# The variance matmul of a fused middle stage, moved behind the first tile of the block's second feed-forward product

## What is computed

```python
# end of layer 0
X = Q + ctx @ W_o
h = relu(X @ w1.T + b1)
x = h @ w2.T + b2 + X            # the kernel's y
# beginning of layer 1
mu = mean(x, axis=-1)
var = mean(square(x - mu), axis=-1)
q = ((x - mu) * rsqrt(var + 1e-5) * gamma + beta) @ Wq.T
```

## Time and profile before

| | |
|---|---|
| median of three runs | 6007.33 us |
| profiled execution | 6018.56 us, span of its trace 6016.6 us |
| busy share of the span: TensorE, VectorE, ScalarE, GpSimd | 92%, 63%, 53%, 44% |
| `middle` in the trace | from about 1741 us to 2137 us |
| mean granted TensorE clock | 0.956 |

### The profile page before, as it was taken

One profiled execution on the slowest core, in us unless ns is written; L12 is line 12 of the kernel. 1 busy time (PEld: TensorE's weight loads), 2 busy tenths in 40 slices (PEclk: granted clock), 3 DMA queues, 4 the chain that ended last, 5 costly groups with the idle time before them and its releaser, 6 DMA issues. The chain is left out here.

```text
span 6016.6 us, 104478 instructions
## 1 busy us (share of the span) xinstructions
PE 5513.0 (92%) x28932; PEld 3458.3 (57%) x28932; DVE 3760.4 (63%) x6550; ACT 3171.1 (53%) x5833; POOL 2621.9 (44%) x1284
## 2 busy tenths in 40 slices
PE   5959999999979979999999999999999995489999
PEld 4834444444437746666565656656566663367877
DVE  4448887778846667777777777777777773511111
ACT  3327776667743346666666666666666662122222
POOL 0000000000000049999999999999999992000000
PEclk9969998999989989999999999999999997799999
DMA  3441111111124321111111111111111115710000
GB/s 107 119 110 29 32 35 32 33 32 36 28 78 124 107 65 40 39 29 38 40 40 40 39 38 30 40 38 39 41 40 28 40 26 161 237 37 14 28 28 14
DMA packets 322981, 323.19 MB, mean 54 GB/s; under 512 B 183136, under 2 KB 187104, under 8 KB 320480
## 3 DMA queue, kind: packets, MB, share of 16 engines
q1 hardware_dynamic: 322528, 317.82, 20.1%
HBM read 210.79 MB, written 106.82 MB: 53 GB/s over the span
## 5 line engine op out<-in xcount | busy, mean ns | idle before, releaser
L750 DVE TENSOR_REDUCE a_maxes<-a_mscore 128x1 f32<-128x458 f32 (+4 forms) x5632 | 3052.8, 605 | 1031.1 <-PE a_mscore L787 1025.7
L733 ACT ACTIVATE a_prob<-a_score 128x512 f32<-128x512 f32 x4992 | 2595.9, 604 | 1402.2 <-PE a_score L796 1391.0
L787 PE MATMUL a_mscore<-a_k,a_qm 96*128 96x458 f32 (+4 forms) x5632 | 2074.6, 416 | 68.8 <-DMA a_k<-k 56.4
L796 PE MATMUL a_score<-a_q,a_k 97*128 97x512 f32 (+1 forms) x4992 | 2061.9, 436 | 76.4 <-ACT a_prob L733 51.8
L703 POOL TENSOR_TENSOR a_added<-a_added,a_prob 128x1024 f32<-128x1024 f32 x768 | 1831.9, 2385 | 90.5 <-ACT a_prob L733 34.1
L787 PEld LDWEIGHTS a_mscore<-a_k,a_qm 96*128 96x128 f32 (+1 forms) x5632 | 1577.7, 309 | 213.8 <-DVE a_maxes L750 92.5
L815 PE MATMUL a_acc<-a_prob,a_v 128*32 128x512 f32 x9984 | 1617.6, 611 | 0.0
L796 PEld LDWEIGHTS a_score<-a_q,a_k 97*128 97x128 f32 (+1 forms) x4992 | 948.9, 194 | 1133.8 <-ACT a_prob L733 599.1
L700 POOL TENSOR_TENSOR a_added<-a_prob 128x1024 f32<-128x1024 f32 x128 | 304.6, 2380 | 2267.6 <-ACT a_prob L733 2267.3
L810 PE MATMUL a_acc<-a_prob,a_ones 128*1 128x512 f32 x2048 | 965.2, 593 | 0.0
L1118 DVE TENSOR_TENSOR f_hl<-f_h,f_hh 128x512 fp32r<-128x512 f32 x128 | 88.6, 692 | 588.0 <-ACT f_hh L1097 588.0
(11 more groups left out here) (183 smaller groups left out, 3842.9 us busy)
## 6 DMA issues: line engine op xcount, KB each, us to landing
a_qm<-q SPq DMA_DIRECT2D x384, 64.0 KB, 1.9
a_q<-q SPq DMA_DIRECT2D x384, 64.0 KB, 1.9
acc<-a_acc_sb SPq DMA_DIRECT2D x384, 64.0 KB
o_part<-acc SPq DMA_DIRECT2D x24, 1024.0 KB, 10.8
a_k<-k SPq DMA_DIRECT2D x48, 416.0 KB, 5.8
q<-m_qout SPq DMA_DIRECT2D x128, 128.0 KB, 2.3
k<-kv_out SPq DMA_DIRECT2D x30, 512.0 KB, 2.7
a_qm<-q SPq DMA_DIRECT2D x384, 32.0 KB, 1.8
```

Of the source, the lines that this page charges most:

```text
L733: act.activation(prob[:, t], score[SCORES[it.j][t]][:], ACT.Exp, scale=SCALE).then_inc(exp_done, 1)
L750: dve.tensor_reduce(maxes[j][:, t, c:c + 1], mscore[u % UNIT_BANKS][:, 0:wide], AX.X, ALU.max).then_inc(unit_read, 1)
L787: pe.matmul(mscore[u % UNIT_BANKS][:, 0:wide], qm[j][r:r + ROW, t:NB:NB // P], kt[kk][r:r + ROW, at:at + wide], start=True, stop=True).the ...
L796: pe.matmul(score[SCORES[it.j][t]][:], kt[it.k][r:r + C, i * P:(i + 1) * P], qt[it.j][r:r + C, :], start=True, stop=True).then_inc(score_d ...
```

## The change

In TensorE's program `project` takes a list of tiles. The first tile of `project(n)` is issued directly behind `hidden(n)`; the waits for `sqsum_done` and for the square root of the block before, and the variance matmul, follow it; then the other three tiles. The other engines' programs are untouched.

```diff
-            def project(n):
+            def project(n, tiles):
                 if n == 0:
                     pe.wait_ge(w_lo, 3)
-                for d in range(KT):
+                for d in tiles:
                     products(prod[d], W2, d, (lambda k: hh[:, k], lambda k: hl[:, k]), HT,
                              (lambda k: pe.wait_ge(hl_done, n * HT + k + 1)) if d == 0 else None).then_inc(c_done, 1)
...
                     hidden(n)
+                if n < BLOCKS:
+                    project(n, [0])
                 if n > 0:
                     pe.wait_ge(sqsum_done, n)
...
                     average(var, sqsum).then_inc(var_done, 1)
                 if n < BLOCKS:
-                    project(n)
+                    project(n, range(1, KT))
                 if n + 1 < BLOCKS:
                     attended(n + 1)
```

## The result

Measured beside the kernel before: 5980.76 us, the median of 15 runs (5974.43 to 5999.6), against 5998.8 us (15 runs, 5991.04 to 6018.08). The ratio is 0.9968, with a 95% interval of 0.9957 to 0.9980: 12 to 26 us faster, where 13.0 was forecast. Two later comparisons of the same pair gave 0.9987 (0.9976 to 0.9999) and 0.9972 (0.9958 to 0.9985); the changed kernel's medians there, 5985.88 and 5983.76 us, lie inside the range.

A forecast was written before the change was run, and what follows sets the result against it. TensorE's work plus two gaps per block of `middle` was taken as the bound. Blocks 2 and 4 (2.4), 1 (1.1), 7 (1.45) and 3, 5, 6 (8.1) sum to 13.0 us: 6007.3 to 5994.3 us, range 5981 to 6006.

The forecast's parts named there:

- Parts 1 and 2: TensorE in `middle`: nine matmuls fill the first gap, a 1.15 us wait remains; TensorE's own gain is 1.4 to 1.5 us.
- two prices: Cost of the moved variance on TensorE: 0.86 us, like the mean matmul, or 0.97 us, as after an idle.
- Part 3: Variance about 1.4 us later costs nothing in VectorE's reciprocal; block 7's starts some 0.6 us later, its end still TensorE's.
- the cover: Time left between the square root's end and the reciprocal that needs it on VectorE: 2.2 us.
- Part 4: At the last `finish`, VectorE's queue is late next, by 0.3 us, capping the gain at 1.18 us in block 2.
- Part 5: TensorE's three falls to 1.2 GHz behind the 2.6 us gap (blocks 3, 5, 6) go, gaining 2.70 us each.
- Rival (a): The falls of TensorE's clock in `middle` stay: gain 9.3 us, 5998.0 us; chance 0.18.
- the sum that the prediction had put beside that remark: Gain in `middle` with the three falls left in: 2.4 + 1.1 + 1.45 + 3 x 1.45 = 9.3 us.
- Rival (d): Slower: attention 1's lower-clock stretch lasts 72 us, not 48, costing 15 us; +2 us net, 6009 us; chance 0.06.
- I put the same difference to the median: The forecast 13.0 us, taken from the profiled execution, is subtracted from the median: 6007.3 - 13.0 = 5994.3 us.

## Which steps of the prediction held, and which missed

- **Parts 1 and 2, the slots.** Right. Nine matmuls, a wait, three, the variance. The wait was 1.36 - 0.23 = 1.13 us against 1.15 forecast; the variance took the lower of its two prices, 0.86 us.
- **Part 3, the cover.** Right: in block 2 the reciprocal did not move, and the two later places of the variance put the price where the cover said it would be. In block 7, without `normalise`, it did wait for the square root, 0.44 us (0.6 forecast), and the last y tile was still idle 2.06 us for TensorE, as forecast.
- **Part 4, who is late next.** Right, VectorE by 0.33 us (0.3 forecast); 1.18 us a block. Without this step, from TensorE's slots alone, it would have been 1.5.
- **Part 5, the clock.** Right in sign and in the price of one fall: the falls hang on the gap, more of them the longer it is, and went away with it. Rival (a) is out with 0 of 54. The Trainium skill's remark (page "TensorE: Matmul & The Clock Gate", Part 1) that the number of slow matmuls varies from run to run is made there of the start of a kernel. The traces agree with it for the start of the stage, where block 1's period varied by 1.8 to 1.9 us on either side; and the falls too sat in other blocks, and were three or four, in the profiles of before. But the sum that the prediction had put beside that remark, with the falls left in, was 9.3 us, and the stage gave 14.8 to 15.4. The step that was mis-sized is here: I took the count of one execution, three falls, where nine passes of the stage had 32 in all, 3.6 on average. That is 0.9 us more. The rest of the way from 13.0 to the stage's 14.8 to 15.4 us lies in TensorE's start at the lower clock, in block 1 and around the loop (a period of 42.1 to 44.0 us in block 1 after, 43.3 to 45.1 before), which I had taken as equal on both sides.
- **Rival (d).** The rest of the span behind the stage shows no gain and no loss beyond its own spread of some 10 us.
- **The number.** The step that put the time outside the range was the last one: "I put the same difference to the median". The median of three runs, 6007.3, was high; that of 15 was 5998.8, 8.5 us lower. The range had "some noise of the medians" in it, without a size, although the three runs alone lay 18 us apart; its lower end was 13.3 us under the forecast. 5998.8 - 13.0 = 5985.8 would have been within. On top the first comparison gave some 4 us more than the stage holds, of the size by which the kernel before differed from itself. That the first median fell 0.24 us outside and the two later ones inside is chance.
- **The chances.** Faster by over 0.3% had 0.22, within 0.3% had 0.75. The first comparison was at 0.32%, the others at 0.13 and 0.28%; the stage's 14.8 to 15.4 us are 0.25%. So the gain lies just inside that bound, and the first figure of it just outside.

## What to carry to other kernels

Putting other work ahead of a wait need not remove it: look for what that work itself waits for, here an operand made behind the very step whose result was waited for. Then follow the earlier result to the engine that takes it, whose own queue caps the gain; the taker's idle time just before it is that cap. And when a difference of 0.2% is forecast, measure the stage by itself and several times over: here four passes alone differed by 61.6 us, with runs that lay within 4 us on either side, so 15.4 us a pass to about 1 us, where the whole kernel told anything from 10 to 19.

## What was new about the hardware

TensorE falls to 1.2 GHz behind some idle gaps that are shorter than the fall itself, which lasts about 3 us: behind 2 of 6 gaps of 2.0 us, 2 of 6 of 2.1 us and 32 of 54 of 2.65 us. It fell behind all 12 gaps of 4.2 and 4.8 us, and behind none of 108 at 1.42 us or below. A stage with one gap of 2.65 us in 42 us of dense work lost 1.5 us more in over half of its blocks 2 to 7. And the phases ahead of an edit, with unchanged code, began 28 us apart between executions, twice what the edit was worth.
